# Attention in a four-stage kernel: how eight PSUM banks are shared between row maxima and exponentials

## The reference

```python
kqv = x @ Wqkv + bqkv                       # x is layer-normalized before
scores = jnp.einsum('bsnh,btnh->bnst', k, q) / math.sqrt(HEAD_SIZE)
scores = jnp.triu(scores) + -10000.0 * jnp.tril(ones, k=-1)
attn = jax.nn.softmax(scores, axis=2)       # over the keys
out = jnp.einsum('bnkq,bknh->bqnh', attn, v)
out = out.reshape(b, s, NUM_HEADS * HEAD_SIZE) @ Wo + bo
```

## Time and profile before

| | |
|---|---|
| median of three runs | 1811.92 us |
| span of the profiled execution | 1799.4 us |
| own time of the profiled execution | not given apart; 12.5 us lie between span and median |
| attention, first score matmul to last value matmul | 176.1 to 533 us |
| busy: TensorE, VectorE, ScalarE, GpSimd | 92%, 61%, 39%, 33% of the span |
| L897 exponentials | 384, 167.6 us busy |
| L840 their score matmuls | 384, 141.0 us busy |
| L815 score matmuls of the maxima | 360, 136.2 us busy |
| L940, L944 reductions | 240 and 120, 109.3 and 77.4 us busy |
| L854 value matmuls | 768, 142.1 us busy |

### The profile page before, as it was taken

One profiled execution on the slowest core, in us unless ns is written; L12 is line 12 of the kernel. 1 busy time (PEld: TensorE's weight loads), 2 busy tenths in 40 slices (PEclk: granted clock), 3 DMA queues, 4 the chain that ended last, 5 costly groups with the idle time before them and its releaser, 6 DMA issues. The chain is left out here.

```text
span 1799.4 us, 22628 instructions
## 1 busy us (share of the span) xinstructions
PE 1662.0 (92%) x7201; PEld 1177.9 (65%) x7201; DVE 1103.2 (61%) x2382; ACT 703.2 (39%) x1330; POOL 587.6 (33%) x859
## 2 busy tenths in 40 slices
PE   6997899999989899999967999999699999999995
PEld 5886454555547677777755767677477777777774
DVE  5444766666736778787878567797544444444442
ACT  3211455555552455555442142212044334433442
POOL 3001333433551334444445051121133333333322
PEclk9998799999999999999988999999899999999998
DMA  7344456556623500000010031102799999999994
GB/s 253 115 141 134 139 159 156 160 161 162 164 70 108 188 1 1 1 1 1 1 59 33 0 119 51 47 21 72 254 325 354 338 357 351 345 345 350 353 354 91
DMA packets 120679, 284.83 MB, mean 158 GB/s; under 512 B 23472, under 2 KB 35248, under 8 KB 120304
## 3 DMA queue, kind: packets, MB, share of 16 engines
q1 hardware_dynamic: 106224, 247.71, 40.0%
q0 software_dynamic: 14336, 35.66, 9.0%
HBM read 224.03 MB, written 54.69 MB: 155 GB/s over the span
## 5 line engine op out<-in xcount | busy, mean ns | idle before, releaser
L897 ACT ACTIVATE probs<-bank 128x512 f32<-128x512 f32 (+3 forms) x384 | 167.6, 503 | 185.4 <-PE bank L840 183.9
L2000 POOL DMA_INDIRECT out_x<-e_y,row_out x64 | 104.0, 1626 | 316.4 <-DMA out_x<-e_y,row_out 174.1
L2035 PE MATMUL bank<-w_gate,xgt 128*128 128x352 f32 x512 | 163.7, 463 | 0.0
L2035 PE MATMUL bank<-w_up,xgt 128*128 128x352 f32 x512 | 161.9, 459 | 0.0
L2101 DVE TENSOR_TENSOR e_hidden<-e_silu,bank 128x352 f32<-128x352 f32 x64 | 33.4, 522 | 201.4 <-issue 181.6
L815 PE MATMUL bank<-k_stack,q_stack 96*128 96x512 f32 (+2 forms) x360 | 136.2, 391 | 22.2 <-DMA k_stack<-qk_parts 11.8
L1200 PE MATMUL bank<-ln_xt_hi,gu_codes 128*128 128x512 f32 x352 | 145.6, 414 | 10.8 <-DVE gate_sum L1273 5.3
L854 PE MATMUL bank<-probs,v_ones 128*64 128x512 f32 (+3 forms) x768 | 142.1, 506 | 6.7 <-POOL probs L764 6.7
L940 DVE CUSTOM_DVE_ANT_0 masked_scores<-bank,wide_mask 128x128 bf16<-128x128 f32 (+1 forms) x240 | 109.3, 482 | 63.5 <-PE bank L815 62.8
L840 PE MATMUL bank<-q_stack,k_stack 98*128 98x512 f32 (+3 forms) x384 | 141.0, 382 | 2.1 <-ACT probs L897 1.8
L764 POOL TENSOR_SCALAR_AFFINE_SELECT probs<-probs 128x128 f32<-128x128 f32 x256 | 77.9, 321 | 196.5 <-ACT probs L897 192.4
(11 more groups left out here) (261 smaller groups left out, 3842.2 us busy)
## 6 DMA issues: line engine op xcount, KB each, us to landing
w_gate<-in_w_gate SPq DMA_DIRECT2D x64, 704.0 KB, 6.7
w_up<-in_w_up SPq DMA_DIRECT2D x64, 704.0 KB, 7.8
w_down<-in_w_down SPq DMA_DIRECT2D x64, 512.0 KB, 8.7
q_stack<-qk_parts SPq DMA_DIRECT2D x96, 128.0 KB, 3.8
k_stack<-qk_parts SPq DMA_DIRECT2D x96, 128.0 KB, 4.0
w_down<-in_w_down SPq DMA_DIRECT2D x64, 192.0 KB, 10.0
qk_parts<-qk_stage_hi SPq DMA_DIRECT2D x32, 256.0 KB, 2.0
qk_parts<-qk_stage_lo SPq DMA_DIRECT2D x32, 256.0 KB, 2.3
```

The lines of the kernel that those rows point to most:

```text
L897: act.activation(probs[u % PROBS][:, 0:cols], m.bank[EXPB[u % 3]][:, 0:cols], ACT.Exp, scale=scale).then_inc(exp_ready, 1)
L2000: pool.indirect_dma_start(out=a["out"][:, :], out_offset=bass.IndirectOffsetOnAxis(ap=row_out[e % YS][:, :], axis=0), in_=y[e % YS][:, :], ...
L2035: last = pe.matmul(m.bank[bank[e % 2]][:, 0:F], xt[e % 2][:, k, :], w[e % R][:, k, :], start=(k == 0), stop=(k == KT - 1))
```

## The change

Bank 2 goes from the exponentials to the maxima: four banks for the maxima's scores, two for the exponentials'. The waits follow: a maxima matmul waits for the entry four places before it, an exponential's matmul for the one two places before it. The projection gets a name of its own, `WOB`, for the same three banks. No engine's order of instructions changes.

```diff
-    MAXB, EXPB, OUTB = (0, 1, 7), (2, 3, 4), (5, 6)
+    MAXB, EXPB, OUTB, WOB = (0, 1, 7, 2), (3, 4), (5, 6), (2, 3, 4)
...
-                need(pe, max_bank_read, at - 2)
-                pe.matmul(m.bank[MAXB[at % 3]][:, 0:cols], qs[slot][j][0:ROWS, q * P:(q + 1) * P],
+                need(pe, max_bank_read, at - 3)
+                pe.matmul(m.bank[MAXB[at % 4]][:, 0:cols], qs[slot][j][0:ROWS, q * P:(q + 1) * P],
...
-                need(pe, max_bank_read, at - 2)
-                pe.matmul(m.bank[MAXB[at % 3]][0:4 * QT, 0:P], top[:, :, :, :].rearrange("p j a q -> p (j a q)"), m.ident[:, :],
+                need(pe, max_bank_read, at - 3)
+                pe.matmul(m.bank[MAXB[at % 4]][0:4 * QT, 0:P], top[:, :, :, :].rearrange("p j a q -> p (j a q)"), m.ident[:, :],
...
-                need(pe, exp_ready, u - 2)
-                bank = m.bank[EXPB[u % 3]]
+                need(pe, exp_ready, u - 1)
+                bank = m.bank[EXPB[u % 2]]
...
-                product3(pe, m.bank[EXPB[t % 3]][:, :],
+                product3(pe, m.bank[WOB[t % 3]][:, :],
...
-                act.activation(probs[u % PROBS][:, 0:cols], m.bank[EXPB[u % 3]][:, 0:cols], ACT.Exp,
+                act.activation(probs[u % PROBS][:, 0:cols], m.bank[EXPB[u % 2]][:, 0:cols], ACT.Exp,
...
-                bank, part = m.bank[MAXB[at % 3]], parts[p % 2][:, j, half, q:q + 1]
+                bank, part = m.bank[MAXB[at % 4]], parts[p % 2][:, j, half, q:q + 1]
```

More of the change, by code:

```diff
@@ L961, in copy_max @@
                     dve.wait_ge(max_placed[(p - 2) % SLOTS], 64 * ((p - 2) // SLOTS + 1))
-                dve.tensor_copy(top_t[p % 2][:, :], m.bank[MAXB[place["turn", p] % 3]][0:4 * QT, 0:P]).then_inc(max_bank_read, 1)
+                dve.tensor_copy(top_t[p % 2][:, :], m.bank[MAXB[place["turn", p] % 4]][0:4 * QT, 0:P]).then_inc(max_bank_read, 1)
             def maxima(entries):
@@ L1006, in _ @@
                 dve.wait_ge(projected, t + 1)
-                dve.tensor_tensor(m.x[:, t, :], m.x[:, t, :], m.bank[EXPB[t % 3]][:, :],
+                dve.tensor_tensor(m.x[:, t, :], m.x[:, t, :], m.bank[WOB[t % 3]][:, :],
                                   ALU.add).then_inc(x_added, 1)
```

## The result

The changed kernel takes 1829.83 us (median of 5 runs, 1825.42 to 1838.42) against 1811.92 before (by now five runs, 1809.47 to 1818.39). The ratio is 1.0099, with a 95% interval of 1.0069 to 1.013. That is 17.9 us slower; the forecast was +12, 1824 us. The direction and most of the mechanism were right, and the sum fell short.

What follows compares the result with a forecast made beforehand. TensorE was taken as the bound, waiting in rounds for VectorE or ScalarE to release banks. Steady pairs 7.2, next to last 1.7, last 2.1 and loads 1 gave +12 us, 1824; range 1813 to 1831 for 8 in 10.

Steps and rivals of the forecast that it cites:

- The rule of the release and the two-bank loop: Exponentials' banks: released 0.05 us after ScalarE's full row ends, so one bank's loop takes 1.15 us for two exponentials.
- Sum of the steady pairs: Full attention pairs: rounds 2 and 3 together +0.29 us, 14 times; rounds 0 and 1 +0.24, 13 times; 7.2 us.
- The last pair: Last attention pair, which has only exponentials: its four rounds grow by 0.7, 0.45, 0.65 and 0.3, together 2.1 us.
- The last but one pair: Next to last attention pair, with half as many maxima: +0.65, -0.3, +0.6 and +0.8 us by rounds, together 1.7.
- +0.8: Round 3 of the next to last pair: last maximum 0.8 us later, delaying the turned maxima, their store and what follows.
- The stack loads: Waits for the k stack in the steady part: 12 waits grow by 0.1 us each, 1 us in all.
- The clock rival: Round 2's longer gaps lower TensorE's clock in each pair, slowing value matmuls: 20 us on top, 1844; chance 6%.
- clock 1.00 in the last pair before: Last pair of the kernel before: gaps in every round yet full clock, taken as evidence that gaps do not lower it.
- The faster rival: Rounds 3, 1 and 0: the maxima's bank is worth more than the exponentials', -0.6 us a pair, 1803; chance 8%.
- E's price: Exponentials' matmuls waiting for ScalarE with one bank fewer: +0.64 us in round 2 and +0.38 in round 0.
- M's gains: Maxima matmuls no longer waiting for VectorE with a fourth bank: -0.35 us in round 3 and -0.14 in round 1.
- The step from span to median: Profiled span 1799.4 to median 1811.92: the 12.5 us around the span or between executions, taken as unchanged.

Runs made afterwards that it cites:

- the earlier load: Changed kernel (four maxima banks, two exponential banks) with SyncE loading the stacks ahead of the stores of the sums' reciprocals: 1818.12 us, 1.0044 of before.
- the bias moved too: Changed kernel with stack loads issued ahead of the reciprocals' stores, and GpSimd's output bias additions moved two pairs ahead: 1811.6 us, 1.0017 of before.

## Why the prediction was right or wrong, point by point

- **The rule of the release and the two-bank loop: right.** 1.15 us for two exponentials was built from rows, 1.18 was measured. Each undisturbed round came within 0.07 us of its replay, and the run with three and two banks shows the two halves of it separately.
- **Sum of the steady pairs: right.** 7.2 us forecast; by the measured rounds 14 x (0.69 - 0.36) + 13 x (0.35 - 0.12) = 7.6.
- **The last pair: right.** 2.1 us forecast; its four rounds rose by 0.64, 0.53, 0.69 and 0.27.
- **The last but one pair: too small.** 1.7 forecast, 3.8 measured (0.65 - 0.29 + 0.69 + 2.73). The step that failed is "+0.8" for its round 3: I moved the last maximum 0.8 us later, which it did, and left the durations behind it as they were. The join, from the start of L950 to the end of L955, took 1.30 us before and 3.25 after: it now falls under GpSimd's L553 and bias additions, and its three small instructions took 0.80, 1.12 and 1.19 us. The sign was in the trace before, beside L553, and I had passed over it:

```profile
508.14 0.76 DVE L955 SCALAR_TENSOR_TENSOR neg_max<-max_parts,neg_max 128x16 fp32r<-128x16 f32 x1
```

- **The stack loads: neither shown nor refuted.** +1 us was forecast. The sums of lateness are 5.7 and 8.8 us at three and three banks, 8.9 and 7.4 at four and two; a growth of 1 us is lost in that. TensorE's waits for the k stack tell no more: 11.7 and 17.1 us in the two profiles of the kernel before, 17.1 and 14.3 in those of the kernel after.
- **The clock rival: partly right, though for another reason.** It was given 6% as an effect of each pair's gaps. In the full pairs the gaps alone did nothing to it (14 of 14 value stretches at full clock with the earlier load, and 14 of 14 with the bias moved too). Behind a late stack the lower clock cost 0.5 to 1.9 us a time: against before, the value stretches behind round 2 took 6.5 us more in the first profile and 0.1 more in the second. Two more slow stretches, 1.7 us each, stand in the last pair of both, with no stack to wait for; the forecast had taken clock 1.00 in the last pair before as a sign against this rival. This part was missing from the sum, and it varies from run to run: with the earlier load alone both are at full clock.
- **The faster rival: its figure does not follow.** A third of E's price, 0.34 us, against M's gains of 0.49 gives -0.15 us a pair, 1810, and not -0.6 and 1803.
- **The step from span to median: right, by what it left open.** Of the 12.5 us, 1.7 lie around the span and the rest between executions. Adding the difference to a median was the right thing to do only because the rest of the 12.5 is spread of the executions and falls on both kernels.
- **Together.** Forecast +12, measured +17.9 with an interval of some 12 to 24 us. By what the profiles bear out: 7.6 + 3.8 + 2.1 = 13.5, and the clock between 3.5 and 9.9 (0.1 to 6.5 behind round 2, and 1.7 twice in the last pair), that is 17.0 to 23.4. The whole is consistent with the measured difference; the split of the last part is not pinned down.

## What to carry to other kernels

Where matmuls of two kinds take turns on one engine, and two engines empty their banks, replay each round for each split from three durations: matmul to reader, the reader's full row, and row end to next weight load. A bank's loop goes by the reader's full row and not by its step, and the busy share shows none of it. And when a replay moves an instruction later, look at what runs on the other engines at its new time: this one met GpSimd there.

## What the runs showed that was not expected

- A 16-column VectorE instruction of 0.17 us takes 1.12 to 1.18 us beside GpSimd's 512-column additions, and one of 704 columns, beside them and the masks behind them, up to 2.64 in place of 0.58. Two 512-column reductions out of PSUM beside the same additions took 1.29 us together, as ever.
- A wait for a transfer of 1.5 us left the clock alone at three and three banks; at four and two, where the round has further gaps of 0.2 to 0.5 us, waits of 0.58 us and more were followed by slow value matmuls in nine of 15 cases (granted clock 0.57 in the one shown). That the gaps are the reason is not shown.
- Of two executions of one kernel, 5.6 us of an 11.0 us difference lay in phases behind the one under study. A difference of two spans should be split by phase before it is explained.
- An idea that was only a probe has the lowest median here: the stack loads issued ahead of the reciprocals' stores, three and three banks, 1801.15 us, 0.9943 of before (0.9919 to 0.9968).
